# A ViT block on one core: the kernel-v product of two images accumulates in one PSUM bank per output block, 196 columns at a time

## The chip, the cores and the metric

The kernel runs on one core of a Trainium2 chip. The metric is the device time of one execution in microseconds (us), the median of several runs. The engines are TensorE (PE, with its weight loads apart as PEld), VectorE (DVE), ScalarE (ACT), GpSimd (POOL) and SyncE (SP), which issues the transfers.

## What is computed

64 images of 3x224x224 are cut into 196 patches each. Cut to what matters here, L = 196, D = 256, S = 128, E = 512:

```
h  = patches @ W.T + b                                 # 196 x 256 per image
x  = layernorm(h)
uv = silu(rmsnorm(x) * g @ uv_w.T)                     # u: 512, v: 512, base: 128
q, k = rope(base * gamma + beta)                       # two of each
kernel = square(relu((q @ k.T + w_rel[idx]) / sqrt(S)))  # 196 x 196 per image
out = (u * (kernel @ v)) @ o_w.T
h  = h + x * res_scale + out
h  = h + ffn(layernorm(h))                             # 8 trees of depth 7: silu(logits) masked by the path
```

`kernel @ v`, the kernel-v product, and the multiplication with `u`, the gate, are what the change touches.

## The kernel before

The work is 32 units of two images; a unit's activations lie as features x 392 tokens (196 of each image). Float32 accuracy comes from three products of `float32r` parts: a value is split into a high part (ACT, `high`) and a low part (DVE, `low`, line 564), and `product` (lines 897 to 901) issues low x high, high x low and high x high, each with a weight load of its own.

Each engine runs a body that is written out by hand: `body(i, n)` interleaves the tree network of unit i with the front (embedding, norms, attention) of unit n = i + 1. The first body has a front only, then come 31 bodies with both in a loop, and the last body has trees only. The attention, and with it the kernel-v product, so runs 32 times, once alone. On each engine the instructions run in the order of that body; semaphores join the engines. The names after the product: `tree_logits`, `tree_visits` and `tree_out` are the three matmul groups of a tree.

The front uses two PSUM banks, `front[:, 0]` and `front[:, 1]`, in turn. The kernel-v product has eight steps per unit, for each of four blocks e of 128 output features and each of two images m. The kernel's 196 keys are two halves of 98 (`HALF`), so a block needs both halves j = 0, 1. `kern_parts[:, m, j]` holds the high and the low part of the kernel side by side, 2 x 196 columns. `mix` (lines 1012 to 1031) streams both parts in one matmul of 392 columns with `v_hi` as weights, twice, and the high part alone, 196 columns, with `v_lo`, twice:

```
pe.matmul(bank[:, 0:2 * L], v_hi[:, 2 * m, at], both[0], start=True, stop=False)
pe.matmul(bank[:, 0:L], v_lo[:, 2 * m, at], kern_parts[:, m, 0, 0], start=False, stop=False)
pe.matmul(bank[:, 0:L], v_lo[:, 2 * m + 1, at], kern_parts[:, m, 1, 0], start=False, stop=False)
pe.matmul(bank[:, 0:2 * L], v_hi[:, 2 * m + 1, at], both[1],
          start=False, stop=True).then_inc(mixed, 1)
```

The bank then has two halves that are still to be added. ACT copies the right one to SBUF (`copy_mix`, line 426), DVE adds the left one to it (`sum_mix`, line 706), and after both images DVE multiplies the sum with `u` (`gate`, line 713). ACT takes the high part of the result (`mix_high`), DVE the low part (`mix_low`), and `project_o` multiplies with `o_w`. PE's order around it is: `tree_visits(5)`, steps 0 and 1, `tree_logits(6, 0)`, steps 2 and 3, `tree_logits(6, 1)`, steps 4 and 5, `tree_out(3, 0)`, steps 6 and 7, `tree_out(3, 1)`, `tree_logits(7, 0)`, `project_o`. A step waits until the sum two steps before has been made, since it takes that bank.

In the first body, which has no trees, `split_late` (line 781) splits the last weights as they arrive: pieces on DVE, others on POOL, each after its transfer.

Of the kernel before, what the change touches and what calls it, by code (L numbers as in the profile page):

```python
# [24 lines left out]
ALU = mybir.AluOpType  # L25
ACT = mybir.ActivationFunctionType
# [7 lines left out]
L = GRID * GRID  # L34
PAIR = 2
T = PAIR * L
# [7 lines left out]
S = 128  # L44
E = 512
EC = E // P
# [18 lines left out]
BANK_V = (1, 0, 1, 0)  # L65
BANK_U = (1, 0, 1, 0)
BANK_QK = (1, 0)
BANK_KV = (1, 0) * EC
BANK_O = (1, 0)


# [11 lines left out]
def vit_tower(nc, x, cols, tok_w, uv_w, o_w, in_w, out_w, rel, rope, anc, ident_in, out):  # L83
    ctx = ExitStack()
    with ctx:
# [3 lines left out]
        def sem(name):  # L89
            return ctx.enter_context(nc.semaphore(name))  # L90
# [35 lines left out]
        base = sb("base", [P, T], F32)  # L126
        base_sw = sb("base_sw", [P, T], F32)
# [3 lines left out]
        v_hi = sb("v_hi", [HALF, GROUPS, E], F32R)  # L131
# [9 lines left out]
        mix_hi = xn[:, :, :, :].rearrange("p a c t -> p (a c) t")  # L141
        mix_lo = qk[:, :, :, :].rearrange("p a c t -> p (a c) t")

        mix_sum = [base, base_sw]
        u_t = u[:, :].rearrange("p (e t) -> p e t", e=EC)
        hid_t = hid[:, :].rearrange("p (s b t) -> p s b t", s=2, b=2)

# [47 lines left out]
        u_ready, u_ok = sem("u_ready"), sem("u_ok")  # L195
        scores_ready, biased, squared = sem("scores_ready"), sem("biased"), sem("squared")
        kern_hi_ok, kern_lo_ok = sem("kern_hi_ok"), sem("kern_lo_ok")
        mixed, mix_copied, summed, gated = sem("mixed"), sem("mix_copied"), sem("summed"), sem("gated")
        mix_hi_ok, mix_lo_ok = sem("mix_hi_ok"), sem("mix_lo_ok")
        projected, h_updated = sem("projected"), sem("h_updated")  # L200
        ffn_x_turned, ffn_x_hi_ok, ffn_x_lo_ok = sem("ffn_x_turned"), sem("ffn_x_hi_ok"), sem("ffn_x_lo_ok")
# [134 lines left out]
        def _(act):  # L336
# [78 lines left out]
                act.wait_ge(squared, PAIR * n + m + 1)  # L415
                high(kern_parts[:, m, :, 0], kern[:, m], kern_hi_ok)

            def copy_mix(n, step):

                if n is None:  # L420
                    return
                e, m = step // PAIR, step % PAIR
                act.wait_ge(mixed, EC * PAIR * n + step + 1)
                if m == 0 and e >= 2:
                    act.wait_ge(gated, EC * n + e - 1)
                act.activation(mix_sum[e % 2][:, m * L:(m + 1) * L], front[:, BANK_KV[step], L:2 * L],
                               ACT.Copy).then_inc(mix_copied, 1)

            def mix_high(n, e):
                if n is None:  # L430
                    return
# [41 lines left out]
            def body(i, n):  # L473
                x_high(n, 0)
                x_high(n, 1)
                silu_tree(i, 0, 1)
                x_high(n, 2)
                silu_tree(i, 0, 0)
                x_high(n, 3)
                x_high(n, 4)  # L480
                x_high(n, 5)
                if first(n):
                    uv_high((0,))
                silu_tree(i, 1, 1)
                hid_high(i, 0)
                silu_tree(i, 1, 0)
                copy_h(n, 0)
                copy_h(n, 1)
                if first(n):
                    uv_high((1, 2))  # L490
                hid_high(i, 1)
                silu_tree(i, 2, 1)
                silu_tree(i, 2, 0)
                silu_tree(i, 3, 1)
                silu_tree(i, 3, 0)
                make_xn(n, 0)
                make_xn(n, 1)
                make_xn(n, 2)
                make_xn(n, 3)
                xn_high(n, 0)  # L500
                xn_high(n, 1)
                hid_high(i, 2)
                silu_base(n)
                hid_high(i, 3)
                silu_v(n, 0)
                silu_v(n, 1)
                v_high(n, 0)
                v_high(n, 1)
                qk_high(n, 0)
                silu_v(n, 2)  # L510
                silu_v(n, 3)
                qk_high(n, 1)
                silu_tree(i, 4, 1)
                silu_u(n, 0)
                silu_tree(i, 4, 0)
                silu_u(n, 1)
                v_high(n, 2)
                silu_tree(i, 5, 1)
                silu_tree(i, 5, 0)
                kern_high(n, 0)  # L520
                v_high(n, 3)
                kern_high(n, 1)
                silu_u(n, 2)
                silu_u(n, 3)
                copy_mix(n, 0)
                copy_mix(n, 1)
                hid_high(i, 4)
                copy_mix(n, 2)
                copy_mix(n, 3)
                mix_high(n, 0)  # L530
                silu_tree(i, 6, 1)
                copy_mix(n, 4)
                mix_high(n, 1)
                copy_mix(n, 5)
                copy_mix(n, 6)
                mix_high(n, 2)
                copy_mix(n, 7)
                silu_tree(i, 6, 0)
                mix_high(n, 3)
                hid_high(i, 5)  # L540
                silu_tree(i, 7, 1)
                silu_tree(i, 7, 0)
                hid_high(i, 6)
                hid_high(i, 7)
                ffn_x_high(n, 0)
                ffn_x_high(n, 1)
                keep_h(n)
# [14 lines left out]
        def _(dve):  # L562
# [133 lines left out]
                dve.wait_ge(kern_hi_ok, PAIR * n + m + 1)  # L696
                low(kern_parts[:, m, :, 1], kern[:, m], kern_parts[:, m, :, 0], kern_lo_ok)

            def sum_mix(n, step):

                if n is None:
                    return
                e, m = step // PAIR, step % PAIR
                dve.wait_ge(mix_copied, EC * PAIR * n + step + 1)
                part = mix_sum[e % 2][:, m * L:(m + 1) * L]
                dve.tensor_tensor(part, front[:, BANK_KV[step], 0:L], part, ALU.add).then_inc(summed, 1)

            def gate(n, e):

                if n is None:  # L710
                    return
                dve.wait_ge(summed, PAIR * (EC * n + e + 1))
                dve.scalar_tensor_tensor(u_t[:, e], mix_sum[e % 2][:, :], 1.0 / S, u_t[:, e],
                                         ALU.mult, ALU.mult).then_inc(gated, 1)

            def mix_low(n, e):
# [68 lines left out]
            def body(i, n):  # L785
# [58 lines left out]
                    split_late(3)  # L844
                mask(i, 4)
                mask(i, 5)
                sum_mix(n, 0)
                sum_mix(n, 1)
                gate(n, 0)
                hid_low(i, 4)  # L850
                sum_mix(n, 2)
                sum_mix(n, 3)
                gate(n, 1)
                decisions(i, 6)
                sum_mix(n, 4)
                mix_low(n, 0)
                sum_mix(n, 5)
                gate(n, 2)
                if first(n):
                    split_late(4)  # L860
                mix_low(n, 1)
                sum_mix(n, 6)
                mix_low(n, 2)
                sum_mix(n, 7)
                gate(n, 3)
                decisions(i, 7)
                mix_low(n, 3)
# [28 lines left out]
        def _(pe):  # L896
# [112 lines left out]
                                   [qk[:, p, 1, at] for p in range(2)], q, True, True)  # L1009
                last.then_inc(scores_ready, 1)  # L1010

            def mix(n, step):


                if n is None:
                    return
                e, m = step // PAIR, step % PAIR
                if step == 0:
                    pe.wait_ge(kern_lo_ok, PAIR * (n + 1))
                if step < 2:  # L1020
                    pe.wait_ge(u_ok, EC * n + step + 3)
                else:
                    pe.wait_ge(summed, EC * PAIR * n + step - 1)
                bank = front[:, BANK_KV[step]]
                at = slice(e * P, (e + 1) * P)
                both = [kern_parts[:, m, j].rearrange("p a l -> p (a l)") for j in range(2)]
                pe.matmul(bank[:, 0:2 * L], v_hi[:, 2 * m, at], both[0], start=True, stop=False)
                pe.matmul(bank[:, 0:L], v_lo[:, 2 * m, at], kern_parts[:, m, 0, 0], start=False, stop=False)
                pe.matmul(bank[:, 0:L], v_lo[:, 2 * m + 1, at], kern_parts[:, m, 1, 0], start=False, stop=False)
                pe.matmul(bank[:, 0:2 * L], v_hi[:, 2 * m + 1, at], both[1],  # L1030
                          start=False, stop=True).then_inc(mixed, 1)

            def project_o(n, m, es):

                if n is None:
                    return
                if first(n) and es[0] == 0:
                    pe.wait_ge(pool_late_lo, 1)
                    pe.wait_ge(dve_late_lo, 1)
                if m == 0 and es[0] == 0:  # L1040
                    pe.wait_ge(summed, EC * PAIR * n + EC * PAIR - 1)
                pe.wait_ge(mix_lo_ok, EC * n + es[-1] + 1)
                for e in es:
                    last = product(front[:, BANK_O[m], 0:T],
                                   [p[:, e, m * P:(m + 1) * P] for p in (o_hi, o_lo)],
                                   (mix_hi[:, e], mix_lo[:, e]), e == 0, e == EC - 1)
                if es[-1] == EC - 1:
                    last.then_inc(projected, 1)
# [39 lines left out]
            def body(i, n):  # L1088
# [45 lines left out]
                tree_out(i, 2, 1)  # L1134
                tree_visits(i, 5)
                mix(n, 0)
                mix(n, 1)
                tree_logits(i, 6, 0)
                mix(n, 2)
                mix(n, 3)  # L1140
                tree_logits(i, 6, 1)
                mix(n, 4)
                mix(n, 5)
                tree_out(i, 3, 0)
                mix(n, 6)
                mix(n, 7)
                tree_out(i, 3, 1)
                tree_logits(i, 7, 0)
                project_o(n, 0, range(0, 3))
# [107 lines left out]
```

## Time and profile before

| | |
|---|---|
| median of 3 runs | 2283.66 us (2283.63 to 2283.84) |
| profiled execution: span | 2279.8 us |
| PE busy | 2216.3 us (97%), 12992 matmuls |
| PEld busy | 2080.7 us (91%), 12992 weight loads |
| DVE busy | 1800.4 us (79%) |
| ACT busy | 1154.4 us (51%) |
| POOL busy | 252.6 us (11%) |
| mean granted clock of TensorE | 0.991 |
| chain that ended last | PE 85%, DVE 8%, issue 3%, ACT 2%, DMA 1% |

The profiled execution has no total time of its own on record beside its span; the median of the runs is 3.9 us above the span (2283.66 against 2279.8), which is what lies before the first and behind the last instruction. Busy time is the union of the durations of an engine's instructions. The durations of matmuls overlap: where they follow each other without a break, the time that one costs is read from start to start, not from its duration.

### The profile page before, as it was taken

The page shows a single profiled execution, that of the slowest core. Times are in us where ns is not written, and L with a number is a line of the kernel's source. Part 1 is how long each engine was busy: PE and PEld are TensorE (multiplying, and loading weights), DVE is VectorE, ACT ScalarE, POOL GpSimd, SP SyncE. Part 2 cuts the span into 40 slices and gives each one's busy share as a digit, 9 for nine tenths or more (in the row PEclk, how much of TensorE's full clock was granted, in tenths as well). Part 3 has the DMA queues.
Part 4 walks back from the last instruction along what each step waited for, and adds up shares of the span by engine and source line. Part 5 has one row for each costly group of instructions (what it writes and reads, how often), then busy time and mean ns, then how long its engine had stood idle before and what let it go on. Part 6 is the DMA issues. An engine that isn't in the chain of part 4 may idle for free.

```text
span 2279.8 us, 37943 instructions
## 1 busy us (share of the span) xinstructions
PE 2216.3 (97%) x12992; PEld 2080.7 (91%) x12992; DVE 1800.4 (79%) x3539; ACT 1154.4 (51%) x2248; POOL 252.6 (11%) x221
## 2 busy tenths in 40 slices
PE   5799999999999999999999999999999999999998
PEld 4799999999999999999999999999999999999998
DVE  6688887788887788877888877888778888778885
ACT  3355554555554555544555545555545555445453
POOL 4101111001111001110011110011100011100110
PEclk8899999999999999999999999999999999999999
DMA  3100000000000000000000000000000000000000
GB/s 126 56 29 7 21 28 28 28 28 0 28 28 28 28 17 11 28 28 28 28 2 26 28 28 28 24 4 28 28 28 28 12 16 28 28 28 28 0 18 15
DMA packets 36667, 58.79 MB, mean 26 GB/s; under 512 B 4174, under 2 KB 29744, under 8 KB 36656
## 3 DMA queue, kind: packets, MB, share of 16 engines
q1 hardware_dynamic: 36656, 58.65, 8.6%
q8 instruction: 6, 0.10, 0.0%
q14 instruction: 5, 0.04, 0.0%
HBM read 45.79 MB, written 12.85 MB: 26 GB/s over the span
## 4 chain that ended last, share of the span: by engine, by line
PE 85%; DVE 8%; issue 3%; ACT 2%; DMA 1%; POOL 0%; SPq 0%; DVEq 0%; ACTq 0%; POOLq 0%
PE front L899 8%; PE front L901 8%; PE front L900 8%; PE hid_ps L899 8%; PE out_acc L899 8%; PE hid_ps L900 8%; PE hid_ps L901 8%; PE out_acc L901 8%; PE out_acc L900 8%; PE hid_ps L1071 4%; PE front L934 3%; PE front L927 2%; DVE tok_major L658 2%; PE front L1030 2%; DVE tok_major L237 2%
## 5 line engine op out<-in xcount | busy, mean ns | idle before, releaser
L462 ACT ACTIVATE hid<-hid_ps,col 128x392 f32<-128x392 f32 x512 | 284.9, 583 | 281.4 <-PE hid_ps L901 227.8
L899 PE MATMUL hid_ps<-ffn_x,in_lo 128*128 128x392 f32 x1024 | 366.9, 358 | 1.2 <-DVE ffn_x L564 1.2
L899 PE MATMUL out_acc<-hid_hi,outw_lo 128*128 128x392 f32 x1024 | 365.9, 357 | 0.0
L900 PE MATMUL hid_ps<-ffn_x,in_hi 128*128 128x392 f32 x1024 | 351.2, 343 | 0.0
L901 PE MATMUL hid_ps<-ffn_x,in_hi 128*128 128x392 f32 x1024 | 350.2, 342 | 0.0
L901 PE MATMUL out_acc<-hid_hi,outw_hi 128*128 128x392 f32 x1024 | 349.0, 341 | 0.0
L900 PE MATMUL out_acc<-hid_lo,outw_hi 128*128 128x392 f32 x1024 | 348.9, 341 | 0.0
L748 DVE SCALAR_TENSOR_TENSOR hid<-hid_ps,hid 128x784 f32<-128x784 f32 x256 | 248.4, 970 | 64.2 <-PE hid_ps L1071 64.2
L307 POOL TENSOR_TENSOR inv_root<-to_root,minus_half 98x8 f32<-98x8 f32 x64 | 106.7, 1668 | 1629.8 <-DVE to_root L604 920.1
L338 ACT ACTIVATE hid_hi<-hid 128x784 fp32r<-128x784 f32 x256 | 218.7, 854 | 132.7 <-PE out_acc L901 116.9
L564 DVE TENSOR_TENSOR hid_lo<-hid,hid_hi 128x784 fp32r<-128x784 f32 x256 | 247.3, 966 | 22.4 <-ACT hid_hi L338 22.4
L899 PEld LDWEIGHTS out_acc<-hid_hi,outw_lo 128*128 128x128 f32 x1024 | 192.7, 188 | 10.8
L899 PEld LDWEIGHTS hid_ps<-ffn_x,in_lo 128*128 128x128 f32 x1024 | 193.8, 189 | 6.2 <-DVE ffn_x L564 1.5
L900 PEld LDWEIGHTS out_acc<-hid_lo,outw_hi 128*128 128x128 f32 x1024 | 193.0, 189 | 1.5
L900 PEld LDWEIGHTS hid_ps<-ffn_x,in_hi 128*128 128x128 f32 x1024 | 194.2, 190 | 0.0
L901 PEld LDWEIGHTS hid_ps<-ffn_x,in_hi 128*128 128x128 f32 x1024 | 193.3, 189 | 0.0
L901 PEld LDWEIGHTS out_acc<-hid_hi,outw_hi 128*128 128x128 f32 x1024 | 192.6, 188 | 0.2
L564 DVE TENSOR_TENSOR x_lo<-x_raw,x_hi 128x392 fp32r<-128x392 f32 x192 | 105.6, 564 | 97.1 <-ACT x_hi L338 97.1
L740 DVE TENSOR_SCALAR decide<-hid_ps,col 128x392 bf16<-128x392 f32 x256 | 156.2, 620 | 29.6 <-PE hid_ps L901 26.2
L899 PE MATMUL front<-xn,uv_lo 128*128 128x392 f32 x320 | 121.5, 380 | 26.3 <-ACT v_full L392 25.8
L625 DVE TENSOR_SCALAR tok_major<-front,moments,inv_root 98x256 f32<-98x256 f32 x256 | 121.4, 536 | 31.8 <-POOL inv_root L307 31.8
L899 PE MATMUL front<-x_hi,tok_lo 128*128 128x392 f32 x384 | 136.3, 355 | 7.2 <-DVE tok_lo L564 7.2
(121 smaller groups left out, 4790.3 us busy)
## 6 DMA issues: line engine op xcount, KB each, us to landing
x_raw<-x SPq DMA_DIRECT2D x192, 196.0 KB, 2.4
out<-out_stage SPq DMA_DIRECT2D x32, 392.0 KB, 2.4
hid<-in_w SPq DMA_DIRECT2D x8, 256.0 KB, 3.1
hid<-out_w SPq DMA_DIRECT2D x8, 256.0 KB, 3.4
tok_major<-tok_w SPq DMA_DIRECT2D x3, 256.0 KB, 4.2
u<-uv_w SPq DMA_DIRECT2D x1, 576.0 KB, 5.1
hid<-o_w SPq DMA_DIRECT2D x2, 256.0 KB, 6.0
h_kept<-uv_w SPq DMA_DIRECT2D x1, 288.0 KB, 5.4
```

The source lines that it names most:

```text
L307: pool.tensor_tensor(inv_root[:, 0:size], to_root[:, 0:size], minus_half[:, 0:size], ALU.pow).then_inc(roots_ok, 1)
L338: act.activation(out, src, ACT.Copy).then_inc(done, 1)
L462: act.activation(hid_t[:, t % 2, b], hid_ps[:, t % 2, b, 0:T], ACT.Silu, bias=c(COL_B_IN + 2 * t + b)).then_inc(activated, 1)
L564: dve.tensor_tensor(out, src, hi.bitcast(F32), ALU.subtract).then_inc(done, 1)
L625: dve.tensor_scalar(normed[:, g], turned(g // 2)[:, g % 2], moments[:, 4, g:g + 1], inv_root[:, g:g + 1], ALU.subtract, ALU.mult).then_inc ...
L740: dve.tensor_scalar(decide[:, t % 2], hid_ps[:, t % 2, 0, 0:T], c(COL_B_IN + 2 * t), 0.0, ALU.add, ALU.is_gt).then_inc(decided, 1)
L748: dve.scalar_tensor_tensor(hid_t[:, t % 2], hid_ps[:, t % 2, :, 0:T], 0.0, hid_t[:, t % 2], ALU.is_ge, ALU.mult).then_inc(masked, 1)
L899: pe.matmul(out, w[1], x_parts[0], start=start, stop=False)
L900: pe.matmul(out, w[0], x_parts[1], start=False, stop=False)
L901: return pe.matmul(out, w[0], x_parts[0], start=False, stop=stop)
L934: last = pe.transpose(front[:, m, g * HALF:(g + 1) * HALF], src[:, g, m * P:(m + 1) * P], ident[0:HALF, 0:HALF])
L1071: last = pe.matmul(hid_ps[:, t % 2, b, 0:T], toward[:, b], decide[:, t % 2], start=True, stop=True)
```

## The change

The four matmuls of a step become six, and two steps become one block: per e, for both images m and both halves of the keys j, `product` issues three matmuls of 196 columns, all into the columns of image m of one bank. The order of the blocks among the tree groups on PE stays as it was. `copy_mix` and `sum_mix`, with their semaphores, go; `gate` reads the PSUM bank. A block waits for the gate two blocks before instead of a sum, and `project_o` for gate 2 instead of a sum.

```
-BANK_KV = (1, 0) * EC
+BANK_MIX = (1, 0) * (EC // 2)
...
-            def copy_mix(n, step):
-
-                if n is None:
-                    return
-                e, m = step // PAIR, step % PAIR
-                act.wait_ge(mixed, EC * PAIR * n + step + 1)
-                if m == 0 and e >= 2:
-                    act.wait_ge(gated, EC * n + e - 1)
-                act.activation(mix_sum[e % 2][:, m * L:(m + 1) * L], front[:, BANK_KV[step], L:2 * L],
-                               ACT.Copy).then_inc(mix_copied, 1)
...
-            def sum_mix(n, step):
-
-                if n is None:
-                    return
-                e, m = step // PAIR, step % PAIR
-                dve.wait_ge(mix_copied, EC * PAIR * n + step + 1)
-                part = mix_sum[e % 2][:, m * L:(m + 1) * L]
-                dve.tensor_tensor(part, front[:, BANK_KV[step], 0:L], part, ALU.add).then_inc(summed, 1)
-
             def gate(n, e):
 
                 if n is None:
                     return
-                dve.wait_ge(summed, PAIR * (EC * n + e + 1))
-                dve.scalar_tensor_tensor(u_t[:, e], mix_sum[e % 2][:, :], 1.0 / S, u_t[:, e],
+                dve.wait_ge(mixed, EC * n + e + 1)
+                dve.scalar_tensor_tensor(u_t[:, e], front[:, BANK_MIX[e], 0:T], 1.0 / S, u_t[:, e],
                                          ALU.mult, ALU.mult).then_inc(gated, 1)
...
-            def mix(n, step):
+            def mix(n, e):
...
-                e, m = step // PAIR, step % PAIR
-                if step == 0:
+                if e == 0:
                     pe.wait_ge(kern_lo_ok, PAIR * (n + 1))
-                if step < 2:
-                    pe.wait_ge(u_ok, EC * n + step + 3)
+                if e < 2:
+                    pe.wait_ge(u_ok, EC * n + e + 3)
                 else:
-                    pe.wait_ge(summed, EC * PAIR * n + step - 1)
-                bank = front[:, BANK_KV[step]]
+                    pe.wait_ge(gated, EC * n + e - 1)
                 at = slice(e * P, (e + 1) * P)
-                both = [kern_parts[:, m, j].rearrange("p a l -> p (a l)") for j in range(2)]
-                pe.matmul(bank[:, 0:2 * L], v_hi[:, 2 * m, at], both[0], start=True, stop=False)
-                pe.matmul(bank[:, 0:L], v_lo[:, 2 * m, at], kern_parts[:, m, 0, 0], start=False, stop=False)
-                pe.matmul(bank[:, 0:L], v_lo[:, 2 * m + 1, at], kern_parts[:, m, 1, 0], start=False, stop=False)
-                pe.matmul(bank[:, 0:2 * L], v_hi[:, 2 * m + 1, at], both[1],
-                          start=False, stop=True).then_inc(mixed, 1)
+                for m in range(PAIR):
+                    for j in range(2):
+                        parts = [kern_parts[:, m, j, p] for p in range(2)]
+                        last = product(front[:, BANK_MIX[e], m * L:(m + 1) * L],
+                                       [v[:, 2 * m + j, at] for v in (v_hi, v_lo)], parts,
+                                       j == 0, j == 1)
+                last.then_inc(mixed, 1)
...
-                    pe.wait_ge(summed, EC * PAIR * n + EC * PAIR - 1)
+                    pe.wait_ge(gated, EC * n + EC - 1)
```

The order of PE's instructions in the loop's body, from block e = 0 of the product on, before (lines 1027 to 1030 are the four matmuls of a step):

```order
L1027 MATMUL front<-kern_parts,v_hi 128x392 [waits u_ok,kern_lo_ok]
L1028 MATMUL front<-kern_parts,v_lo 128x196
L1029 MATMUL front<-kern_parts,v_lo 128x196
L1030 MATMUL front<-kern_parts,v_hi 128x392
L1027 MATMUL front<-kern_parts,v_hi 128x392 [waits u_ok]
L1028 MATMUL front<-kern_parts,v_lo 128x196
L1029 MATMUL front<-kern_parts,v_lo 128x196
L1030 MATMUL front<-kern_parts,v_hi 128x392
```

And of the changed kernel (lines 862 to 864 are its `product`):

```order
L862 MATMUL front<-kern_parts,v_lo 128x196 [waits u_ok,kern_lo_ok]
L863 MATMUL front<-kern_parts,v_hi 128x196
L864 MATMUL front<-kern_parts,v_hi 128x196
L862 MATMUL front<-kern_parts,v_lo 128x196
L863 MATMUL front<-kern_parts,v_hi 128x196
L864 MATMUL front<-kern_parts,v_hi 128x196
L862 MATMUL front<-kern_parts,v_lo 128x196
L863 MATMUL front<-kern_parts,v_hi 128x196
L864 MATMUL front<-kern_parts,v_hi 128x196
L862 MATMUL front<-kern_parts,v_lo 128x196
L863 MATMUL front<-kern_parts,v_hi 128x196
L864 MATMUL front<-kern_parts,v_hi 128x196
```

Eight matmuls of a block, four of them with 392 columns, are now twelve of 196; the wait between the two images is gone.

DVE's order in the loop's body, from the second mask (`mask(i, 5)`) on, before:

```order
L748 SCALAR_TENSOR_TENSOR hid<-hid_ps,hid 128x784 [waits visits_ready]
L704 ISA
L706 TENSOR_TENSOR base<-front,base 128x196 [waits mix_copied]
L704 REGISTER_ALU
L706 TENSOR_TENSOR base<-front,base 128x196 [waits mix_copied]
L712 REGISTER_ALU
L713 SCALAR_TENSOR_TENSOR u<-base,u 128x392 [waits summed]
L564 TENSOR_TENSOR hid_lo<-hid,hid_hi 128x784 [waits hid_hi_ok]
```

And of the changed kernel:

```order
L719 SCALAR_TENSOR_TENSOR hid<-hid_ps,hid 128x784 [waits visits_ready]
L684 SCALAR_TENSOR_TENSOR u<-front,u 128x392 [waits mixed]
L544 TENSOR_TENSOR hid_lo<-hid,hid_hi 128x784 [waits hid_hi_ok]
L684 SCALAR_TENSOR_TENSOR u<-front,u 128x392 [waits mixed]
L710 ISA
L711 TENSOR_SCALAR decide<-hid_ps,col 128x392 [waits logits_ready]
```

The sums ahead of each gate are gone, and the gate waits for PE itself.

## Rows read from the trace of the kernel before

**Rows 1.** Page: busy time of each engine, and the chain that ended last.

```profile
PE 2216.3 (97%) x12992; PEld 2080.7 (91%) x12992; DVE 1800.4 (79%) x3539; ACT 1154.4 (51%) x2248; POOL 252.6 (11%) x221
PE 85%; DVE 8%; issue 3%; ACT 2%; DMA 1%; POOL 0%; SPq 0%; DVEq 0%; ACTq 0%; POOLq 0%
```

**Rows 2.** Waits of PE: us in total, times, longest us.

```profile
PE front L899 <- ACT v_full L392: 25.8, 32, 6.6
...
PE front L899 <- DVE qk L564: 4.8, 1, 4.8
...
PE front L1027 <- DVE base L706: 0.5, 2, 0.2
```

**Rows 3.** Timeline, PE and PEld, one block of the product: start, duration.

```profile
1170.38 0.34 PE L1027 MATMUL front<-kern_parts,v_hi 98*128 98x392 f32 x1
...
1170.56 0.25 PE L1028 MATMUL front<-kern_parts,v_lo 98*128 98x196 f32 x1
1170.56 0.19 PEld L1029 LDWEIGHTS front<-kern_parts,v_lo 98*128 98x128 f32 x1
1170.65 0.27 PE L1029 MATMUL front<-kern_parts,v_lo 98*128 98x196 f32 x1
1170.67 0.19 PEld L1030 LDWEIGHTS front<-kern_parts,v_hi 98*128 98x128 f32 x1
...
1170.76 0.36 PE L1030 MATMUL front<-kern_parts,v_hi 98*128 98x392 f32 x1
1170.78 0.19 PEld L1027 LDWEIGHTS front<-kern_parts,v_hi 98*128 98x128 f32 x1
1170.96 0.34 PE L1027 MATMUL front<-kern_parts,v_hi 98*128 98x392 f32 x1
...
1171.54 0.34 PE L899 MATMUL hid_ps<-ffn_x,in_lo 128*128 128x392 f32 x1
```

**Rows 4.** Timeline, PE and PEld, first and last of six score matmuls.

```profile
1162.02 0.25 PE L899 MATMUL front<-qk 128*98 128x196 f32 x1
1162.02 0.16 PEld L900 LDWEIGHTS front<-qk 128*98 128x98 f32 x1
...
1162.47 0.25 PE L901 MATMUL front<-qk 128*98 128x196 f32 x1
```

**Rows 5.** Groups by line and form, ACT's copies and DVE's sums.

```profile
L426 ACT ACTIVATE base<-front 128x196 f32<-128x196 f32 x128 | 42.4, 331 | 56.1 <-PE front L1030 56.1
```

```profile
L706 DVE TENSOR_TENSOR base<-front,base 128x196 f32<-128x196 f32 x128 | 46.0, 360 | 12.2 <-ACT base L426 12.1
L639 DVE SCALAR_TENSOR_TENSOR hT<-front,col,hT 128x392 f32<-128x392 f32 x64 | 40.1, 626 | 16.3 <-PE front L934 16.3
L713 DVE SCALAR_TENSOR_TENSOR u<-base_sw,u 128x392 f32<-128x392 f32 x64 | 37.1, 579 | 2.2
```

**Rows 6.** Timeline, PE and DVE, around the first sums and gate of a unit.

```profile
1168.00 0.48 PE L1027 MATMUL front<-kern_parts,v_hi 98*128 98x392 f32 x1
...
1168.34 0.97 DVE L748 SCALAR_TENSOR_TENSOR hid<-hid_ps,hid 128x784 f32<-128x784 f32 x1 [0.30 <-PE hid_ps L1071]
...
1170.27 0.57 DVE L713 SCALAR_TENSOR_TENSOR u<-base,u 128x392 f32<-128x392 f32 x1
```

**Rows 7.** Timeline, ACT, DVE and PE, the chain to `make_u(n, 0)`.

```profile
1151.50 0.50 ACT L384 ACTIVATE base<-front 128x392 f32<-128x392 f32 x1 [2.98 <-PE front L901]
...
1158.46 0.53 ACT L338 ACTIVATE qk<-tok_major 128x392 fp32r<-128x392 f32 x1 [1.50 <-DVE tok_major L239]
1159.13 1.20 ACT L392 ACTIVATE v_full<-front 98x512 f32<-98x512 f32 x2
```

**Rows 8.** Timeline, DVE and PE, end of the product in the first body.

```profile
60.97 0.58 DVE L713 SCALAR_TENSOR_TENSOR u<-base,u 128x392 f32<-128x392 f32 x1
...
61.47 1.49 DVE L781 CAST outw_hi<-hid 128x512 fp32r<-128x512 f32 x1
...
66.66 0.66 PE L899 MATMUL front<-xn,o_lo 128*128 128x392 f32 x1 [4.82 <-DVE qk L564]
```

More of the change, by code:

```diff
@@ L142, in vit_tower @@
         mix_lo = qk[:, :, :, :].rearrange("p a c t -> p (a c) t")
-        mix_sum = [base, base_sw]
         u_t = u[:, :].rearrange("p (e t) -> p e t", e=EC)
@@ L197, in vit_tower @@
         kern_hi_ok, kern_lo_ok = sem("kern_hi_ok"), sem("kern_lo_ok")
-        mixed, mix_copied, summed, gated = sem("mixed"), sem("mix_copied"), sem("summed"), sem("gated")
+        mixed, gated = sem("mixed"), sem("gated")
         mix_hi_ok, mix_lo_ok = sem("mix_hi_ok"), sem("mix_lo_ok")
@@ L524, in body @@
                 silu_u(n, 3)
-                copy_mix(n, 0)
-                copy_mix(n, 1)
                 hid_high(i, 4)
-                copy_mix(n, 2)
-                copy_mix(n, 3)
                 mix_high(n, 0)
                 silu_tree(i, 6, 1)
-                copy_mix(n, 4)
                 mix_high(n, 1)
-                copy_mix(n, 5)
-                copy_mix(n, 6)
                 mix_high(n, 2)
-                copy_mix(n, 7)
                 silu_tree(i, 6, 0)
@@ L846, in body @@
                 mask(i, 5)
-                sum_mix(n, 0)
-                sum_mix(n, 1)
                 gate(n, 0)
                 hid_low(i, 4)
-                sum_mix(n, 2)
-                sum_mix(n, 3)
                 gate(n, 1)
                 decisions(i, 6)
-                sum_mix(n, 4)
                 mix_low(n, 0)
-                sum_mix(n, 5)
                 gate(n, 2)
@@ L861, in body @@
                 mix_low(n, 1)
-                sum_mix(n, 6)
                 mix_low(n, 2)
-                sum_mix(n, 7)
                 gate(n, 3)
@@ L1136, in body @@
                 mix(n, 0)
+                tree_logits(i, 6, 0)
                 mix(n, 1)
-                tree_logits(i, 6, 0)
+                tree_logits(i, 6, 1)
                 mix(n, 2)
+                tree_out(i, 3, 0)
                 mix(n, 3)
[L1141 to L1146, printed above, removed]
                 tree_out(i, 3, 1)
```

## The prediction

> **What bounds the kernel now.** I read the busy shares first, then who waits for whom, then the timeline of one block of the product. PE is busy for 97% of the span and its weight loads for 91%, DVE for 79% and ACT for 51%; the chain that ended last is 85% PE [rows 1]. PE's waits say where anything but PE decides. Only one wait comes back in every body: the first `make_u` matmul (line 899) waits for ACT's `v_full`, 25.8 us in 32 times, of which 6.6 us is one long one in the first body, so about 19.2 / 31 = 0.62 us each. At the product itself PE waits for a sum twice, 0.5 us, both in the first body [rows 2]. So in 31 of 32 units PE runs through the product without a stop, and whatever the change does to DVE and ACT there shortens nothing that PE is waiting for. What PE issues there counts in full.
>
> **PE's part: twelve short matmuls for eight.** The columns are the same: before, per block, 4 x 392 + 4 x 196 = 2352, after 12 x 196 = 2352. What differs is how weight loads fit beside them. Every matmul has a load of its own, and the timeline shows what a short matmul costs with it. In a block before, the start of `L1027` to that of the next group is 1171.54 - 1170.38 = 1.16 us for 8 matmuls; a 392-column one whose successor's load is covered takes 0.18 us from start to start. The two short ones in the middle show the limit: the load for `L1029` starts at 1170.56, that for `L1030` at 1170.67, the next at 1170.78, so loads of 128 weight columns follow each other at 0.11 us and no faster, though the short matmul before one of them took only 0.09 us from start to start. And the 392-column `L1030` after them takes 0.20 us instead of 0.18: the lag comes back there [rows 3].
>
> The contrast is the scores: also 196 columns a matmul, but with weights of 98 columns. Six of them stand 0.45 us apart from the first to the last, 0.09 us each, and a load takes 0.16 instead of 0.19 us [rows 4]. So 0.09 us is what 196 moving columns cost, 0.11 us what a load of 128 weight columns costs, and the larger of the two sets the pace. The product's weights, `v_hi` and `v_lo`, have 128 columns.
>
> Sum for a block after: 12 x 0.11 = 1.32 us, against 1.16: **+0.16 us**. (The same arithmetic gives the block before: four long at 0.18 and four short at 0.11 is 1.16 us, which is what the timeline has.) There are 4 blocks x 32 units = 128 of them: 128 x 0.16 = **+20.5 us**. The pace is read to 0.01 us; from 0.108 to 0.112 us it makes 1.30 to 1.34 us a block, +17.4 to +23.6 us (with a block before of 1.16).
>
> The Trainium skill, "TensorE: Matmul & The Clock Gate", section "LDWEIGHTS (loading the stationary operand)", has a load cost its columns divided by 1.2, in ns, whatever the rows: 107 ns for 128 columns and 82 ns for 98. By that estimate a block would take 1.28 us and the term be +15.4 us. It speaks against the change as the rows do; the measured 0.11 us is the value taken.
>
> **DVE and ACT.** ACT loses eight copies of 331 ns a unit, 2.6 us, and DVE eight sums of 360 ns, 2.9 us. The gate reads PSUM instead of SBUF: the same kind of instruction with a PSUM source of 392 columns takes 626 ns where the gate takes 579, so four gates grow by 0.19 us [rows 5]. In the 31 bodies with trees I cost all of this at nothing, gain and loss alike. PE's own queue is the cover: the instructions that follow the product on PE don't wait for its results before, and get them earlier now.
>
> **The new waits.** The gate of block 0 stands behind the second mask on DVE, which ends at 1169.31; block 0's first matmul starts at 1168.00 and lasts 0.48 instead of 0.34 us, since it is queued 0.14 us behind the visits, so the block now ends at about 1168.14 + 1.32 = 1169.5 and gate 0 at about 1170.3, where it ended at 1170.84 before [rows 6]. Block 2, which needs its bank, starts on PE only after `tree_logits(6, 0)`, block 1 and `tree_logits(6, 1)`: 6 x 0.18 + 1.32 + 6 x 0.18 = 3.5 us behind the end of block 0, at about 1173.0. That leaves 2.7 us of slack. Gate 1 is queued behind `hid_low(4)`, which waits for ACT's high part; ACT has lost the two copies that stood ahead of that. It has 3.5 us as well. `project_o` waits for gate 2, and two tree groups (2.2 us) stand between. Cost: nothing. If that cover were gone, a late gate would show at the first matmul of blocks 2 and 3.
>
> **The 0.62 us that PE waits at `make_u`.** It is earlier in the body than the product. The chain there starts from PE: base on ACT at 1151.50, then nothing but DVE and ACT until ACT is through with `qk` at 1158.46 and takes `v_full` at 1159.13 [rows 7]. ACT had waited 2.98 us for PE at its start, so both engines are in step with PE there and carry no backlog over from the product. It stays.
>
> **The first body.** There are no trees to cover anything. Sums are on the path, and PE waits 4.8 us before `project_o`, for DVE, which has gate 2 at 60.97, then splits a late weight at 61.47 and resumes the products late [rows 8]. Without copies and sums gate 2 could start about 1 us sooner, and two sums of 0.36 us fall away between it and the low parts that `project_o` needs. The weight that is split may not have landed by then (no wait for it shows before), so the gain lies between 0.4 us and 2.5 us; I take **-1.0 us**, nearer to the two sums, which are certain.
>
> **Sum:** +20.5 - 1.0 = +19.5 us on the profiled execution, 2279.8 to 2299.3 us of span; the runs lie 3.9 us above the span, so 2283.66 + 19.5 = **2303 us**. A measurement of this kernel can tell 0.2%, 4.6 us, from no change.
>
> **Rivals.**
>
> Columns decide, not loads (faster). If the 0.02 us lag behind a short matmul were a matter of switching between lengths, twelve equal short ones would run at the scores' 0.09 us: 1.08 us a block, 128 x (1.08 - 1.16) = -10.2 us, with the first body 2272 us. For it: the start of `L1029` follows `L1028` by 0.09 us. Against it: the loads' own starts are 0.11 us apart twice in a row, and the lag is not lost but paid at the next long matmul [rows 3]. It decides from the point where a 128-column load can start less than 0.09 us behind the one before. The same page of the Trainium skill, section "Back-to-back issue gap", gives a lone matmul N / 2.4 + 2.5 ns, 84 ns for 196 columns, which would have this sign; it says itself that streams with loads are set by both. Chance 4%.
>
> The time that DVE and ACT save reaches PE (no change). If the 0.62 us at `make_u` came from a backlog that starts in the product, 5.5 us less work would remove it: 31 x 0.62 = -19.2 us, and the kernel would stay at about 2284 us. Against it stands ACT's 2.98 us of idle time just before [rows 7]. Chance 4%.
>
> A new wait takes the place (slower still). If gates come late for their banks, because `hid_low(4)` holds gate 1 until ACT delivers, each of blocks 2 and 3 could stand for the length of a gate, 0.6 us: 31 x 2 x 0.6 = +37 us, about 2340 us. The slack of 2.7 us speaks against it. Chance 3%.
>
> The forecast, loads at 0.11 us and all else covered: 89%.
>
> **How the numbers follow.** The forecast's own range is the pace of 0.108 to 0.112 us with a first body of -2.5 to -0.4 us: +14.9 to +23.2 us, 2298.6 to 2306.9 us. I widen it a little for the rounding of the block before, to 2296 and 2309 us. The other cases are rarer than 2 in 10 together and stay outside. Faster is the first rival, 4%, and a rest of 1%; same the second, 4%; slower everything else, 91%.
>
> **What the changed profile should show.** 1024 x 1.5 matmuls for the product (1536 for 1024, 13504 in all), their loads 0.11 us apart; a block of 1.32 us from its first matmul to the next group's; DVE busy down by 92 - 6 = 86 us and ACT by 85 us; PE's wait at `make_u` as before, no wait at the product. Loads at 0.09 us would make the prediction wrong towards faster; PE waits on the gate (line 684) towards slower; a smaller wait at `make_u` would say that the second rival holds.

## The result, and the profile after

| | kernel before | changed kernel |
|---|---|---|
| median | 2283.64 us (2283.46 to 2283.84, 4 runs) | 2302.52 us (2301.60 to 2303.28, 4 runs) |
| profiled execution: time, span | span 2279.8 us | 2302.81 us, span 2300.5 us |

The ratio of the runs is 1.0085 (95% interval 1.0071 to 1.0099): the change makes the kernel 18.9 us slower. The prediction was 2303 us, slower. The two profiled executions lie further apart, by 20.7 us of span, most likely because the one of the kernel before was quicker than its median: the executions of that kernel that have both on record took 2.0 to 2.1 us more than their span, so a span of 2279.8 us belongs to some 2281.9 us, not to 2283.64. The 3.9 us that I gave ahead of the prediction as the time outside the span is therefore too much; the forecast doesn't hang on it, since it adds to the median.

The page of the changed kernel, its busy times, the answer to [rows 1]:

```profile
PE 2237.2 (97%) x13504; PEld 2102.5 (91%) x13504; DVE 1715.5 (75%) x3283; ACT 1091.0 (47%) x1992; POOL 252.4 (11%) x221
```

DVE has 84.9 us less to do, as forecast (86), and ACT 63.4 us less where I had said 85. The copies' durations do add up to 85 us, but a copy overlaps the instruction behind it, and busy time counts that once: in the timeline before, a copy starts at 1173.39, lasts 0.33 us, and the next instruction on ACT starts at 1173.62. PE has 20.9 us more, and the span grew by 20.7 us. PE's waits, the answer to [rows 2] (line 862 here is line 899 before):

```profile
PE front L862 <- ACT v_full L391: 25.8, 32, 6.6
...
PE front L862 <- DVE qk L544: 3.2, 1, 3.2
PE hid_ps L1033 <- ACT hid L450: 2.4, 1, 2.4
...
PE front L862 <- DVE kern_parts L544: 0.8, 1, 0.8
```

The wait at `make_u` is 25.8 us in 32 times, as before, and no wait for a gate is there. The gate of block 0 ends at 1178.70 + 0.57 = 1179.27, and block 2, which needs its bank, starts on PE at 1182.02, 2.75 us later, as forecast (2.7). DVE:

```profile
1178.70 0.57 DVE L684 SCALAR_TENSOR_TENSOR u<-front,u 128x392 f32<-128x392 f32 x1 [0.34 <-PE front L864]
```

The first body's wait before `project_o` fell from 4.8 to 3.2 us.

A block of the product in the timeline of PE and PEld (start, duration), the answer to [rows 3]:

```profile
1179.60 0.25 PE L862 MATMUL front<-kern_parts,v_lo 98*128 98x196 f32 x1
1179.60 0.19 PEld L863 LDWEIGHTS front<-kern_parts,v_hi 98*128 98x128 f32 x1
1179.69 0.27 PE L863 MATMUL front<-kern_parts,v_hi 98*128 98x196 f32 x1
1179.71 0.19 PEld L864 LDWEIGHTS front<-kern_parts,v_hi 98*128 98x128 f32 x1
1179.80 0.28 PE L864 MATMUL front<-kern_parts,v_hi 98*128 98x196 f32 x1
1179.83 0.19 PEld L862 LDWEIGHTS front<-kern_parts,v_lo 98*128 98x128 f32 x1
...
1180.81 0.28 PE L864 MATMUL front<-kern_parts,v_hi 98*128 98x196 f32 x1
1180.83 0.19 PEld L862 LDWEIGHTS hid_ps<-ffn_x,in_lo 128*128 128x128 f32 x1
1180.92 0.37 PE L862 MATMUL hid_ps<-ffn_x,in_lo 128*128 128x392 f32 x1
1180.94 0.19 PEld L863 LDWEIGHTS hid_ps<-ffn_x,in_hi 128*128 128x128 f32 x1
1181.12 0.34 PE L863 MATMUL hid_ps<-ffn_x,in_hi 128*128 128x392 f32 x1
```

The loads start at 1179.60, .71 and .83, one behind the other, and the matmuls follow at their pace. From its first matmul to the next group's is 1.32 us, and that group's first matmul then takes 0.20 instead of 0.18 us: the block costs 1.34 us, against 1.16 before.

One number makes all comparisons below sharp: the **body**, the time from one body's wait at `make_u` to the next one's. In the chain that ended last (start, duration, engine and line), the kernel before:

```profile
1159.78 0.45 PE front L899
...
1229.11 0.45 PE front L899
```

and the changed kernel:

```profile
1168.82 0.45 PE front L862
...
1238.89 0.45 PE front L862
```

69.33 us before, 70.07 us after (within each of these two executions the 30 bodies that can be read in this way agree to 0.04 us). So 0.74 us a body, 0.18 to 0.19 us for each of its four blocks, and 31 x 0.74 = 22.9 us for the loop. The first body goes the other way. Timeline of PE, from its first product matmul to its first tree matmul, before:

```profile
55.22 0.45 PE L1027 MATMUL front<-kern_parts,v_hi 98*128 98x392 f32 x1 [0.82 <-DVE kern_parts L564]
...
82.63 0.69 PE L899 MATMUL hid_ps<-ffn_x,in_lo 128*128 128x392 f32 x1 [1.19 <-DVE ffn_x L564]
```

and after:

```profile
56.45 0.36 PE L862 MATMUL front<-kern_parts,v_lo 98*128 98x196 f32 x1 [0.82 <-DVE kern_parts L544]
...
80.86 0.69 PE L862 MATMUL hid_ps<-ffn_x,in_lo 128*128 128x392 f32 x1 [1.19 <-DVE ffn_x L544]
```

27.4 us became 24.4, 3.0 us less. What lies ahead of the product, with the first transfers, took 1.2 us more in this execution (56.45 against 55.22), though the change touches nothing there; in the profiled executions of the experiments below, whose kernels are alike up to there as well, the product starts between 55.20 (e3) and 56.91 us (e4). 22.9 - 3.0 + 1.2 = 21.1 us, against 20.7 of span. Single executions of one kernel differ by a microsecond or two in this way, which is why the experiments are read by their body first.

### The profile page after: what moved, and what is told of

Its sections match the earlier page's. It is cut to its first block, busy times and chain, and to the rows that moved or that the text cites. A ratio compares the mean times of both kernels' runs of the same rounds, so it can differ in the third digit from the quotient of the medians.

```text
span 2300.5 us, 37678 instructions
## 1 busy us (share of the span) xinstructions
PE 2237.2 (97%) x13504; PEld 2102.5 (91%) x13504; DVE 1715.5 (75%) x3283; ACT 1091.0 (47%) x1992; POOL 252.4 (11%) x221
## 4 chain that ended last, share of the span: by engine, by line
PE 85%; DVE 8%; issue 3%; ACT 2%; DMA 1%; POOL 0%; SPq 0%; DVEq 0%; ACTq 0%; POOLq 0%
PE front L862 11%; PE front L864 10%; PE front L863 10%; PE hid_ps L862 8%; PE out_acc L862 8%; PE hid_ps L863 8%; PE hid_ps L864 8%; PE out_acc L864 7%; PE out_acc L863 7%; PE hid_ps L1033 4%; PE front L897 3%; PE front L890 2%; DVE tok_major L638 2%; DVE tok_major L236 2%; DVE v_lo L544 1%
## 5 line engine op out<-in xcount | busy, mean ns | idle before, releaser
L862 PE MATMUL front<-xn,uv_lo 128*128 128x392 f32 x320 | 121.6, 380 | 26.3 <-ACT v_full L391 25.8
```

Of the source, the lines that this page charges most:

```text
L862: pe.matmul(out, w[1], x_parts[0], start=start, stop=False)
```

## The experiments

Theory: a short matmul with weights of 128 columns costs the load of the next weights, so the twelve cost more than the eight; what ACT and DVE save reaches only the first body. Each run stands beside runs of the kernel before on its own chip: 2283.08 us for e1 to e4, 2282.35 for e5 to e8, 2282.29 for e9.

### e1: weights of 98 columns

```
-                at = slice(e * P, (e + 1) * P)
+                at = slice(e * P, e * P + 98)
...
-                        last = product(front[:, BANK_MIX[e], m * L:(m + 1) * L],
+                        last = product(front[0:98, BANK_MIX[e], m * L:(m + 1) * L],
```

> The changed kernel with weights of 98 columns instead of 128 in the kernel-v product; it leaves out the last 30 of every 128 output features of the product. Moving columns and the number of matmuls stay. Theory (the load of 128 weight columns, 0.111 us, paces the short matmuls): the pace falls to the 0.091 us of the scores, a block from 1.34 to 1.09 us, 128 x 0.24 = 31 us less than the changed kernel, so about 2271 us, below the kernel before (2283.6). Rival (the cost belongs to short matmuls on 98 rows or to accumulating into the same columns): about 2302 us as the changed kernel.

Measured: 2272.51 us (ratio to before 0.9951, 0.9934 to 0.9967). The chain's rows:

```profile
1154.77 0.45 PE front L862
...
1223.91 0.45 PE front L862
```

A body of 69.14 us, 0.93 less than the changed kernel's: 0.23 us a block. The same twelve matmuls with the same 196 moving columns are now cheaper than the eight of before. The time came out 1.5 us above the theory's 2271 us, and the rival's 2302 is out.

The columns of the weights are also the partitions that a matmul writes, so this edit alone doesn't say which of the two sets the pace. The kernel before does, at the start of the product in its first body, where PE had been idle:

```profile
55.22 0.19 PEld L1027 LDWEIGHTS front<-kern_parts,v_hi 98*128 98x128 f32 x1 [1.14 <-DVE kern_parts L564]
...
55.33 0.19 PEld L1028 LDWEIGHTS front<-kern_parts,v_lo 98*128 98x128 f32 x1
55.51 0.25 PE L1028 MATMUL front<-kern_parts,v_lo 98*128 98x196 f32 x1
```

The matmul of `L1028` starts 0.29 us behind that of `L1027`, at 55.22, but its load starts 0.11 us behind the load before it: the 0.11 us are between the loads, also where no matmul keeps that pace.

### e2: 98 moving columns

```
-                        parts = [kern_parts[:, m, j, p] for p in range(2)]
-                        last = product(front[:, BANK_MIX[e], m * L:(m + 1) * L],
+                        parts = [kern_parts[:, m, j, p, 0:HALF] for p in range(2)]
+                        last = product(front[:, BANK_MIX[e], m * L:m * L + HALF],
```

> The changed kernel with 98 moving columns instead of 196 in every matmul of the product, weights of 128 columns as they are; it leaves out half of the queries of every image in the product. Half of the product's column work is gone. Theory (loads pace): the pace stays at 0.111 us, so 2302 us within 2 us. Rival (moving columns set the cost, with some overhead for each matmul): 98 columns less at 0.46 ns is 0.045 us a matmul, 1536 x 0.045 = 69 us less, about 2233 us.

Measured: 2305.63 us (1.0097, 1.0080 to 1.0114). The body, and four rows of PE and PEld from one block:

```profile
1171.07 0.45 PE front L862
...
1241.18 0.45 PE front L862
```

```profile
1181.97 0.19 PEld L864 LDWEIGHTS front<-kern_parts,v_hi 98*128 98x128 f32 x1
1182.02 0.28 PE L864 MATMUL front<-kern_parts,v_hi 98*128 98x98 f32 x1
1182.08 0.19 PEld L862 LDWEIGHTS front<-kern_parts,v_lo 98*128 98x128 f32 x1
1182.13 0.28 PE L862 MATMUL front<-kern_parts,v_lo 98*128 98x98 f32 x1
```

Half of the product's columns are gone and the body is 70.11 us, as with all of them. Loads still start 0.11 us apart. The time is 3.1 us above the changed kernel's, outside the 2 us that I had allowed. About 1 us of it is in the bodies (31 x 0.04), and the first body took 2.6 us more, 27.0 against 24.4. The granted clock was 0.61 in the 10 us from 55 us on, where the product of that body starts, against 0.96 in the changed kernel's from 56 us on. The product started at the higher level, with loads 0.11 us apart, and from 57.2 us on, with PE busy since 55.33, its matmuls followed each other at 0.21 us; from 58 to 63 us the granted clock was 0.50, the lower of the two levels (1.2 GHz). Why it fell in this kernel and not in the changed one was not tried.

### e5: weights of 112 columns

The edit is that of e1 with 112 for 98.

> The changed kernel with weights of 112 columns in the product; it leaves out the last 16 of every 128 output features of the product. Theory (a load costs 0.111 us for 128 columns and in proportion less): 112 / 128 x 0.111 = 0.097 us, still above the 0.091 us of 196 moving columns; 0.014 x 12 x 4 = 0.67 us less for each body than the changed kernel's 70.07, so 69.4 us a body. Rival (a step between two fixed costs): a body as with 98 columns, 69.13 us, or as with 128, 70.07 us.

Measured: 2282.15 us, a single execution, so the body is what counts. Two rows of PEld from one block, a load and the next, and the body:

```profile
1167.37 0.18 PEld L863 LDWEIGHTS front<-kern_parts,v_hi 98*112 98x112 f32 x1
...
1167.47 0.18 PEld L864 LDWEIGHTS front<-kern_parts,v_hi 98*112 98x112 f32 x1
```

```profile
1159.01 0.45 PE front L862
...
1228.51 0.45 PE front L862
```

A body of 69.50 us stands between 69.14 and 70.07, loads 0.10 us apart. So the cost follows the weight columns, not a step between two fixed costs: 0.57 us less than with 128, a little less than the 0.67 expected.

### e6: long, short, long, short

```
-                pe.matmul(bank[:, 0:L], v_lo[:, 2 * m + 1, at], kern_parts[:, m, 1, 0], start=False, stop=False)
-                pe.matmul(bank[:, 0:2 * L], v_hi[:, 2 * m + 1, at], both[1],
+                pe.matmul(bank[:, 0:2 * L], v_hi[:, 2 * m + 1, at], both[1], start=False, stop=False)
+                pe.matmul(bank[:, 0:L], v_lo[:, 2 * m + 1, at], kern_parts[:, m, 1, 0],
                           start=False, stop=True).then_inc(mixed, 1)
```

> The kernel before with the four matmuls of a step in the order long, short, long, short instead of long, short, short, long. Theory (each short matmul costs the load of the next weights, wherever it stands): a block stays at 1.16 us, a body at 69.33 us, the time at 2283 us. Rival (only the second of two short ones in a row is slowed): 128 x 2 x 0.02 to 0.04 = 5 to 10 us less.

Measured: 2282.73 us (1.0001, 0.9991 to 1.0010), a body of 69.34 us. In the timeline:

```profile
1170.53 0.25 PE L1028 MATMUL front<-kern_parts,v_lo 98*128 98x196 f32 x1
...
1170.62 0.37 PE L1029 MATMUL front<-kern_parts,v_hi 98*128 98x392 f32 x1
...
1170.82 0.25 PE L1030 MATMUL front<-kern_parts,v_lo 98*128 98x196 f32 x1
```

Behind a short matmul the long one starts after 0.09 us and its own successor after 0.20 instead of 0.18: a start 0.09 us later is not a cost of 0.09 us. Every short one costs 0.11, wherever it stands.

### e3: the relief of ACT and DVE alone

`copy_mix` and its calls are taken out; each sum becomes half a gate, and the full gate goes:

```
-                dve.wait_ge(mix_copied, EC * PAIR * n + step + 1)
-                part = mix_sum[e % 2][:, m * L:(m + 1) * L]
-                dve.tensor_tensor(part, front[:, BANK_KV[step], 0:L], part, ALU.add).then_inc(summed, 1)
+                dve.wait_ge(mixed, EC * PAIR * n + step + 1)
+                part = u_t[:, e, m * L:(m + 1) * L]
+                dve.scalar_tensor_tensor(part, front[:, BANK_KV[step], 0:L], 1.0 / S, part,
+                                         ALU.mult, ALU.mult).then_inc(summed, 1)
```

> The kernel before with its long and short matmuls as they are, but without ACT's copies and without the sums: in the place of each sum DVE gates the left half of the bank directly, 196 columns. It leaves out the v_hi x kernel-low part of the product, which stands in the right half of the bank. Theory: this is the change's relief of ACT and DVE alone, worth 1 to 3 us in the first body and nothing in the others: 2281 to 2283 us. Rival (the saved time reaches PE's 0.62 us wait at make_u): about 2264 us.

Measured: 2278.80 us (0.9982, 0.9973 to 0.9992), 4.3 us less than before. The chain's rows:

```profile
1156.53 0.45 PE front L869
...
1225.88 0.45 PE front L869
```

The body is 69.35 us, the kernel before's to 0.02 us: ACT and DVE lost 63.4 and 79.2 us of work and the loop gained nothing. The first body took 24.3 us instead of 27.4 (product at 55.20, trees at 79.54), 3.1 us less, nearly the same gain as in the changed kernel (3.0). This is all of the relief's effect that the trace shows; the rest of the 4.3 us lies within what executions differ by.

### e4: the short matmuls alone

`mix` issues two `product`s per step into one bank per block; copies and sums stay, but must wait for the whole block, since one bank now holds both images:

```
-                act.wait_ge(mixed, EC * PAIR * n + step + 1)
+                act.wait_ge(mixed, PAIR * (EC * n + e + 1))
...
-                dve.wait_ge(mix_copied, EC * PAIR * n + step + 1)
+                dve.wait_ge(mix_copied, PAIR * (EC * n + e + 1))
```

> The kernel before with the changed kernel's twelve short matmuls in one bank per block, and ACT's copies and DVE's sums kept (they copy and add the same columns, and the gate halves the doubled sum); copies and sums of a block start when the whole block is done. Theory: PE's part of the change alone, 128 x 0.18 = 23 us, with no gain in the first body: 2305 to 2308 us. Rival (the relief was needed to get 2302.5, or hides more): a larger difference to the changed kernel than the 3 us of the first body, with waits of PE at the product.

Measured: 2315.20 us (1.0139, 1.0122 to 1.0156), more than expected. The body:

```profile
1177.81 0.45 PE front L899
...
1248.14 0.45 PE front L899
```

70.33 us, 0.26 more than the changed kernel's. It arises at `project_o`: up to its first matmul the two kernels' PE keeps the same distances from the start of the product (11.01 and 10.87 us, the first difference), and at the first matmul of its second group, 1198.97 against 1189.73, the difference has grown to 0.27 us. Timeline, DVE and PE:

```profile
1196.33 0.56 DVE L564 TENSOR_TENSOR qk<-u,xn 128x392 fp32r<-128x392 f32 x1
...
1196.71 0.34 PE L901 MATMUL hid_ps<-ffn_x,in_hi 128*128 128x392 f32 x1
...
1197.03 0.42 PE L899 MATMUL front<-xn,o_lo 128*128 128x392 f32 x1
```

`project_o` starts 0.32 us behind the matmul ahead of it instead of 0.18: the low part of block 2 ends at 1196.89. Such a wait is shorter than a matmul's modelled duration, so the view of waits doesn't list it. Here the rival is half right: with short matmuls in one bank, copies and sums that wait for the whole block come late enough to stop PE. The copies' later start is part of this experiment, and it doesn't separate the two; that the change needs the relief is shown for this arrangement alone. The sum closes: 31 x 1.00 us in the bodies and 1.4 us more in the first body (28.8 against 27.4) are 32.4 us over the kernel before, and 32.1 were measured.

### e7 and e8: work for the wait at make_u

On the kernel before, e7 moves one tree group on PE, e8 another:

```
+                tree_logits(i, 5, 1)
                 make_u(n, 0)
                 make_u(n, 1)
                 scores(n, 0)
-                tree_logits(i, 5, 1)
```

```
                 tree_out(i, 2, 0)
+                tree_out(i, 2, 1)
                 make_u(n, 0)
...
                 make_u(n, 3)
-                tree_out(i, 2, 1)
```

> The kernel before with tree_logits(5, 1) moved on PE from between the two scores to ahead of make_u 0, where PE waits 0.62 us in every body. Theory: the wait goes, but scores 1 and make_u 2 lose their cover of 1.07 us and wait for silu_u 1 and for DVE's bias, some 0.2 to 0.6 us; 0 to 0.4 us a body, 2271 to 2283 us. Rival (the cover is needed in full): same or a few us slower.

> The kernel before with tree_out(2, 1) moved on PE from behind make_u 3 to ahead of make_u 0. Theory: the 0.62 us wait goes, and kernel-v block 0, which now follows make_u 3 and the visits at once, waits about as long for the low part of the kernel and for silu_u 2 (cover lost 1.07 us, needed some 0.6 to 0.9 us): within 5 us of the kernel before. Rival: the cover behind make_u 3 is slack, then 19 us less, 2264 us.

Measured: e7 2273.40 us (0.9958, 0.9942 to 0.9975), e8 **2263.17 us** (0.9913, 0.9897 to 0.9930), which is faster than both kernels. The bodies of e8, from the first matmul of one product to that of the next:

```profile
1159.65 0.45 PE L1027 MATMUL front<-kern_parts,v_hi 98*128 98x392 f32 x1
...
1228.36 0.45 PE L1027 MATMUL front<-kern_parts,v_hi 98*128 98x392 f32 x1
```

68.71 us, 0.62 less than before. I had costed the lost cover behind `make_u(3)` at 0.6 to 0.9 us, and the rival in e8's expectation was right: it was slack. From start to start the wait before was longer than listed. Timeline of PE in the kernel before:

```profile
1158.82 0.34 PE L901 MATMUL out_acc<-hid_hi,outw_hi 128*128 128x392 f32 x1
...
1159.78 0.45 PE L899 MATMUL front<-xn,uv_lo 128*128 128x392 f32 x1 [0.62 <-ACT v_full L392]
```

0.96 us for a step that takes 0.18, so 0.78 us of it was waiting, and the matmul behind the wait takes 0.28 us from start to start (1159.78 to 1160.06) instead of 0.18: together 0.88 us. In e8 the steps there are 0.18 us, and all 0.88 us are gone. Of them 0.26 us come back at the product, whose first matmul now starts 0.49 us behind the start of the visits ahead of it (1159.16) where it was 0.20 us, and itself takes 0.29 where it took 0.32: 0.88 - 0.26 = 0.62 us. e7's body is 69.07 us (first product matmuls at 1163.59 and 1232.66): of the 0.62 us some 0.27 are gained.

### e9: the change with e8's order

> The changed kernel with tree_out(2, 1) ahead of make_u 0, as in e8_out_ahead. Theory: the change costs 0.73 us a body there too, and the moved group takes the 0.62 us wait away there too: 2302.5 - 19.3 = 2283 us, the time of the kernel before. Rival (with the wait gone, PE hangs on DVE and ACT at the product, and their relief pays): 2275 us or less.

Measured: 2284.64 us (1.0010, 1.0001 to 1.0020), as the theory said within 2 us. e8 and e9 differ by the change alone: 2284.64 - 2263.17 = 21.5 us in two sets of runs, in which the kernel before agrees within 0.1 us. The first product matmul of one body and of the next in e9:

```profile
1165.82 0.36 PE L862 MATMUL front<-kern_parts,v_lo 98*128 98x196 f32 x1
...
1235.27 0.36 PE L862 MATMUL front<-kern_parts,v_lo 98*128 98x196 f32 x1
```

That is a body of 69.45 us, 0.74 more than e8's 68.71. So the change costs the same 0.74 us a body where PE has no wait left at `make_u`.

## Why the prediction was right

**The bound.** PE through the product without a stop: right. The relief left the loop's body at 69.35 us (e3), and no wait for a gate came up. One reading was short: PE's waits for sums in the first body are three, not two, since `base_sw` has a row of its own beside `base`; it changes nothing in the loop.

**The pace.** 0.11 us for a short matmul with 128 weight columns: right, and the mechanism with it. Weights of 98 and 112 columns lower it (e1, e5), half the moving columns don't (e2), and the order doesn't matter (e6); the two loads of the kernel before shown under e1 tie the 0.11 us to the load and not to what a matmul writes. The size of the term was too small. I took +0.16 us a block, +20.5 us; it is +0.18 us, 128 x 0.18 = 23.0 us, for a pace of 1.34 / 12 = 0.112 us, the upper end of what I had given. I had read 0.11 from rows rounded to 0.01 us, and left out the lag of 0.02 us that [rows 3] show behind a short matmul: it falls on the group that follows the block, 0.20 instead of 0.18 us. The Trainium skill, "TensorE: Matmul & The Clock Gate", section "LDWEIGHTS (loading the stationary operand)", would have had 1.28 us a block. Its rule, that a load goes by its columns, agrees with e5 in its direction; with 98 columns the 196 moving columns set the pace and e1 doesn't show the load's own cost. What the rule gives is below what was measured, 0.107 against 0.112 us for 128 columns and 0.093 against 0.100 for 112, and the measurement decides.

**The first body.** I took -1.0 us, between -0.4 and -2.5; it was -3.0 in the changed kernel and -3.1 in e3, outside that range. Timeline of DVE and PE in the changed kernel, to be read beside [rows 8]:

```profile
60.76 0.57 DVE L684 SCALAR_TENSOR_TENSOR u<-front,u 128x392 f32<-128x392 f32 x1 [0.30 <-PE front L864]
61.24 0.42 DVE L752 CAST outw_hi<-hid 128x512 fp32r<-128x512 f32 x1
...
65.25 0.66 PE L862 MATMUL front<-xn,o_lo 128*128 128x392 f32 x1 [3.19 <-DVE qk L544]
```

| stretch | before | after | less |
|---|---|---|---|
| first product matmul to gate 2 | 5.75 us | 4.31 us | 1.44 us |
| gate 2 to the split | 0.50 us | 0.48 us | 0.02 us |
| the split to `project_o` | 5.19 us | 4.01 us | 1.18 us |
| `project_o` to the first tree matmul | 15.97 us | 15.61 us | 0.36 us |

The earlier gate was meant to be worth about 1 us, and alone was worth 1.44. The two sums of 0.36 us that I called certain are not found behind it: in all 1.18 us went between the split and `project_o`, and 1.07 of them are the split itself, which took 1.49 us before and 0.42 here. That leaves 0.1 us for the sums; the second of them started at 66.43, when the low part that `project_o` waited for was nearly done. So the earlier gate alone brought more than the whole term, the sums that I leaned on brought next to nothing, and the split's length I had put at nothing. Before, the split ran beside a `TENSOR_TENSOR` of POOL's (61.21 to 62.68); in e4 it did so too and took 1.48 us, and in e3, where POOL still stood idle, it took 0.42. That this is the cause was not tried. Behind `project_o` the granted clock was 0.66 in the first 5 us, and 0.58 before, with PE busy throughout; by my estimate that is 5 x 0.08 = 0.4 us, about the 0.36.

**The sum.** In the loop I had 31 x 4 x 0.16 = +19.8 us, and it was +22.9. In the first body I had its four blocks and the relief, 0.6 - 1.0 = -0.4 us, and it was -3.0. Two errors of opposite sign, +3.1 and -2.6 us, nearly cancel, which is luck: the measured terms make +19.9 us where I had +19.5. The medians differ by 18.9 us, and the last 1.0 us is within what executions of one kernel differ by. The total was closer than its terms.

**The new waits and the wait at make_u.** No wait for a gate appeared, and the 0.62 us stayed. The rival that columns decide fell with e2, where half of them made no difference, that the saved time reaches PE with e3. What I did not see is that this wait could be filled by one move that gains 19.2 us, about as much as the change costs (e8).

## What to carry to other kernels

In a kernel like this one, with `float32r` matmuls and a load for each, cost a matmul on a busy TensorE as the larger of its moving columns and the load of the next weights, and read both from start to start: splitting long matmuls at equal column count is not free once a piece is shorter than a load. Where TensorE is the bound, work taken from the other engines pays only where TensorE waits for them; list those places before the change and count the rest at nothing, but see that results don't come later than before, as e4's did. A wait that comes back in every body, even one of 0.6 us, is worth more than 85 us of busy time on an engine that nobody waits for.

## What the runs showed of the hardware

- With 196 moving columns a matmul costs 0.112 us with weights of 128 columns, 0.100 with 112 and 0.092 with 98 (1.34 / 12, and from it the differences of the bodies of 70.07, 69.50 and 69.14 us over a body's 48 matmuls of the product); the scores' 0.09 us [rows 4] agree with the last.
- With 98 moving columns and 128 weight columns it costs the same 0.112 us (70.11 us a body).
- A late start of PE by 0.14 us before `project_o` (e4) is in no list of waits, and the wait listed with 0.62 us is 0.78 us long and costs 0.88 us with the slower matmul behind it (e8), since matmul durations are modelled and overlap; both show only from start to start.
- At the lower level of the clock (granted 0.50) the short matmuls with 128 weight columns followed each other at 0.21 us instead of 0.11 (e2, first body).
- In the rows shown here no weight load starts ahead of the matmul before its own (both at 1170.56 in [rows 3], both at 1179.60 in the changed kernel), and a long matmul gives a short one beside it nothing back: in e6's order the body is 69.34 us as before.
- Where PE had been idle, loads of 128 weight columns still started 0.11 us apart while their matmuls were 0.29 us apart (55.22 us in the kernel before).
